# A second attention of five overlapped sequences: norm, transposes, roundings and maxima moved earlier in the slot, half of the masks on ScalarE

## The reference

```
hn = layernorm(x);  q, k, v = hn @ wq + bq, hn @ wk + bk, hn @ wv + bv      # 16 heads of 8
scores = q k^T / sqrt(8);  attn = softmax(scores);  o = attn @ v
x = x + (o @ wo + bo)
hn2 = layernorm(x);  logits = hn2 @ gate_w + gate_b;  idx = argmax(logits)
```

## Time and profile before

| | us |
|---|---|
| three runs, median (lowest to highest) | 1882.75 (1875.11 to 1886.69) |
| the profiled execution: time, span | 1882.32, 1880.5 |
| second attention, first query/key/value product to the end of its last stage | about 1226 to 1684 of the span |
| mean length of the 12 full slots (1299.6 to 1623.2) | 26.97 |

### The profile page before, as it was taken

The page is one execution under the profiler, slowest core; times in us unless marked ns, Lnnn a source line. Parts: engine busy times, 40 slices in busy tenths (PEclk is TensorE's granted clock), DMA queues, the critical chain, the costliest instruction groups (busy, mean ns, idle before and its releaser), DMA issues.

```text
span 1880.5 us, 28307 instructions
## 1 busy us (share of the span) xinstructions
PE 1255.7 (67%) x8634; PEld 880.8 (47%) x8635; DVE 1244.0 (66%) x2728; ACT 727.4 (39%) x1190; POOL 1018.8 (54%) x1176
## 2 busy tenths in 40 slices
PE   3435333478777777877787779257767776746796
PEld 1223122236666565656665558223433333325685
DVE  6788850177787878787878873167777778743322
ACT  1101001145454454454444553036565555532221
POOL 2356576456666666666666645334445444425554
PEclk7555555578888888888888887669898889878766
DMA  4010004400000000000000000210000000001110
GB/s 132 22 27 15 13 13 81 94 7 1 8 8 8 7 6 6 6 6 6 6 3 3 7 4 6 72 33 12 19 18 16 9 17 17 7 17 44 42 40 12
DMA packets 73354, 40.91 MB, mean 22 GB/s; under 512 B 23811, under 2 KB 68716, under 8 KB 73284
## 3 DMA queue, kind: packets, MB, share of 16 engines
q1 hardware_dynamic: 50530, 24.02, 4.6%
q0 software_dynamic: 20384, 11.67, 3.1%
q10 hardware_dynamic: 2370, 4.35, 0.8%
HBM read 31.11 MB, written 23.87 MB: 29 GB/s over the span
## 4 chain that ended last, share of the span: by engine, by line
PE 33%; DVE 29%; issue 13%; POOL 13%; ACT 7%; DMA 2%; ACTq 1%; POOLq 1%; SPq 0%; DVEq 0%; another core or an unknown queue 0%
PE psum L1138 9%; PE psum L1189 5%; POOL xe_dram L570 4%; DVE terms L1766 4%; DVE o L1606 4%; PE psum L1246 3%; POOL o_inv L618 3%; DVE q_highT L1792 2%; PE psum L1166 2%; POOL got L768 2%; POOL out L777 2%; PE psum L1304 1%; DVE rden L1458 1%; PE psum L1269 1%; DVE silu_g L1700 1%
## 5 line engine op out<-in xcount | busy, mean ns | idle before, releaser
L1138 PE MATMUL psum<-v,attn 128*128 128x64 f32 x2048 | 287.8, 300 | 25.6 <-ACT aggr L870 17.1
L1138 PEld LDWEIGHTS psum<-v,attn 128*128 128x128 f32 x2048 | 271.9, 213 | 61.1 <-issue 44.2
L1766 DVE TENSOR_REDUCE terms<-psum 128x4 bf16<-128x1024 f32 x128 | 156.9, 1226 | 45.5 <-PE psum L1269 43.7
L641 POOL DMA_INDIRECT yg<-ye_dram,routel x128 | 140.1, 1095 | 60.0 <-issue 36.2
L945 ACT ACTIVATE prob<-psum 128x512 f32<-128x512 f32 x256 | 139.5, 602 | 49.7 <-PE psum L1233 45.5
L570 POOL DMA_INDIRECT xe_dram<-rows_out,route x128 | 131.8, 1030 | 39.6 <-issue 39.0
L855 ACT ACTIVATE attn<-psum 128x1024 f32<-128x1024 f32 x128 | 129.9, 1015 | 10.1 <-PE psum L1121 8.9
L1147 PE MATMUL psum<-ident,o 128*128 128x128 f32 x256 | 48.7, 353 | 117.9 <-DVE silu_g L1700 91.0
L618 POOL TENSOR_TENSOR o_inv<-o_max,minus_half 128x16 f32<-128x16 f32 x32 | 107.6, 3364 | 2.7
L658 POOL TENSOR_TENSOR v<-v,inv 128x2048 f32<-128x2048 f32 x16 | 70.7, 4418 | 59.8 <-DVE inv L1586 59.8
L1147 PEld LDWEIGHTS psum<-ident,o 128*128 128x128 f32 x256 | 39.1, 183 | 131.5 <-DVE o L1606 66.5
(11 more groups left out here) (300 smaller groups left out, 3106.5 us busy)
## 6 DMA issues: line engine op xcount, KB each, us to landing
x4n_dram<-x4n SPq DMA_DIRECT2D x16, 256.0 KB, 4.5
w<-in_w POOLq DMA_DIRECT2D x48, 64.0 KB, 2.3
x_in<-in_x SPq DMA_DIRECT2D x8, 256.0 KB, 2.9
xe_dram<-zero_rows SPq DMA_DIRECT2D x8, 256.0 KB, 3.2
x_dram<-x1s SPq DMA_DIRECT2D x8, 256.0 KB, 2.4
xe_dram<-rows_out,route POOLq DMA_INDIRECT x128, 2.1
xe<-xe_dram SPq DMA_DIRECT2D x16, 128.0 KB, 2.4
ye_dram<-ye SPq DMA_DIRECT2D x16, 128.0 KB, 2.2
```

The lines of the kernel that those rows point to most:

```text
L641: pool.indirect_dma_start(yg[fetch.p][:, j, k, :], None, ye_dram, bass.IndirectOffsetOnAxis(ap=where[:, j, K0 + k:K0 + k + 1], axis=0), bo ...
L1138: mm = pe.matmul(psum[:, 4 + j, (head % HALF) * DV:(head % HALF + 1) * DV], attn[g % RING][:, h, c * SEQ + j * P:c * SEQ + (j + 1) * P], v ...
L1766: dve.tensor_reduce(dst[:, :, 2 * m2:2 * m2 + 2], psum[:, 4:6, :].rearrange("q p (b k) -> q p b k", b=2), AX, ALU.max, negate=True).then_i ...
```

## The change

Per slot: the layer norm of the fetched sequence is taken at g 2 and 4 (DVE) in place of 5 and 7, and its transposes and `h4T` at g 5 in place of 7, now in `ring[0]`. On POOL the powers for that norm stand ahead of `end` and `tail`. The query/key/value product stands ahead of the slot's first scores, and so also ahead of `values4(tail, 3)`. DVE adds query and key for both halves first and v after them, and `qkv_out` is now signalled by the v additions. The roundings on ACT stand one g earlier, the transposes of the high parts at g 1, and on DVE the choice of the expert stands in g 1 ahead of the rest, the high copy and the masks. Four of the eight masks are made by ACT at g 2. The maxima run from g 2 on: r = 0, 1, 2, 4, 5, 7 at g 2 to 7, and 3 and 6 as second ones at g 4 and 6. The diff, cut to its core:

```diff
@@ POOL half: the block "if fetch" (inverse_deviation("var4") to x3n_made) moves from behind "if tail" to ahead of "if end"
@@ ACT half
-                    if front and g == 1:
+                    if front and g == 0:
                         act.wait_ge(s["qkv_out"], 2 * front.n)
                         act.activation(high4[:], qk4[:], ACT.Copy).then_inc(s["high4_made"], 1)
-                    if front and g == 2:
+                    if front and g == 1:
                         wait(act, s["q4_ps"], 2 * (front.n - 1))
                         act.wait_ge(s["rest4_made"], front.n)
                         act.activation(flat[:, :, MID, :], qk_flat, ACT.Copy).then_inc(s["mid4_made"], 1)
+                    if front and g == 2:
+                        act.wait_ge(s["high_out"], front.n)
+                        for m in range(HALF // 2, HALF):
+                            act.activation(q_highT[:, m, :], highT[:, 0, :], ACT.Copy, scale=head_mask[:, m:m + 1]).then_inc(s["masked_act"], 1)
+                    if fetch and g == 5:
+                        act.wait_ge(s["x4T_ps"], fetch.n)
+                        act.activation(h4T[:], ring[0][:, 0:SEQ], ACT.Identity, bias=norms[:, 1:2], scale=norms[:, 0:1]).then_inc(s["h4T_made"], 1)
-                    if fetch and g == 7:
-                        act.wait_ge(s["x4T_ps"], fetch.n)
-                        act.activation(h4T[:], ring[1][:, 0:SEQ], ...)
@@ PE half
+                    if front and g == 0:
+                        for j in range(2):
+                            b = fill4(1 - j, [(s["qkv_out"], 2 * (front.n - 1) + j + 1)], [(s["h4T_made"], front.n)] if j == 0 else [])
+                            pe.matmul(b[:, 0:3 * D], h4T[:, j * P:(j + 1) * P], w_qkv[:], start=True, stop=True).then_inc(s["qkv_ps"], 1)
                     if att:
                         scores4(att, g)
                     if tail and g == 0:
                         values4(tail, 3)
-                    if front and g == 0:
-                        ...
-                    if front and g == 2:
+                    if front and g == 1:
                         b16 = fill4(0, [(s["high_out"], front.n)], [(s["high4_made"], front.n)]).bitcast(BF16)
-                    if front and g in (3, 4, 5, 6, 7):
-                        maxima(front, (0, 1, 3, 4, 6)[g - 3])
+                    if front and g > 1:
+                        maxima(front, (0, 1, 2, 4, 5, 7)[g - 2])
+                    if fetch and g == 5:
+                        b = fill4(0, [(s["h4T_made"], fetch.n)], [(s["xn4_made"], fetch.n)])
+                        ...
-                    if fetch and g == 7:
-                        b = fill4(1, [], [(s["xn4_made"], fetch.n)])
-                        ...
-                    if front and g in (4, 6, 7):
-                        maxima(front, {4: 2, 6: 5, 7: 7}[g])
+                    if front and g in (4, 6):
+                        maxima(front, {4: 3, 6: 6}[g])
@@ DVE half
                     if front and g == 0:
-                        wait(dve, s["pv_made"], HEADS * (front.n - 2))
                         wait(dve, s["terms4_made"], 6 * (front.n - 1))
                         for j in range(2):
                             dve.wait_ge(s["qkv_ps"], 2 * (front.n - 1) + j + 1)
+                            chain.step(dve.tensor_tensor(qk4[:, :, j, :], ...))
+                        wait(dve, s["pv_made"], HEADS * (front.n - 2))
+                        for j in range(2):
+                            dve.tensor_tensor(v4[front.p][:, j, :, 0:DH], ...).then_inc(s["qkv_out"], 1)
-                    if end and g == 2:
+                    if end and g == 1:
                         for j in range(2):
                             n = chain.step(dve.max(top_b[:, j, :], logit[:, j, :]))
                         ...
+                    if front and g == 1:
+                        (rest4, highT)
+                        for m in range(HALF // 2):
+                            dve.tensor_scalar(q_highT[:, m, :], highT[:, 0, :], head_mask[:, m:m + 1], None, ALU.mult).then_inc(s["masked"], 1)
+                    if fetch and g == 2:
+                        moments(x3l[fetch.p], stats4, meanvar4, "var4")
+                    if front and g > 1:
+                        take_maxima(front, (0, 1, 2, 4, 5, 7)[g - 2])
+                    if front and g == 4:
+                        take_maxima(front, 3)
+                    if fetch and g == 4:
+                        normed(xn4, x3l[fetch.p], meanvar4, rstd4, "xn4_made")
                     if front and g == 6:
-                        take_maxima(front, 5)
+                        take_maxima(front, 6)
```

More of the change, by code:

```diff
@@ L1300, in half @@
                         values4(tail, 3)
-                    if front and g == 0:
-                        for j in range(2):
-                            b = fill4(1 - j, [(s["qkv_out"], 2 * (front.n - 1) + j + 1)], [(s["h4T_made"], front.n)] if j == 0 else [])
-                            pe.matmul(b[:, 0:3 * D], h4T[:, j * P:(j + 1) * P], w_qkv[:], start=True, stop=True).then_inc(s["qkv_ps"], 1)
                     if att and g == 1:
@@ L1783, in half @@
                         dve.sem_inc(s["logit1_out"], 1)
-                    if front and g == 1:
-                        dve.wait_ge(s["high4_made"], front.n)
-                        dve.tensor_tensor(qk4[:], qk4[:], high4[:], ALU.subtract).then_inc(s["rest4_made"], 1)
-                    if front and g == 2:
-                        dve.wait_ge(s["high_ps"], front.n)
-                        dve.tensor_copy(highT[:].rearrange("q w t -> q (w t)"), ring[0].bitcast(BF16)[:, 0:2 * SEQ]).then_inc(s["high_out"], 1)
-                        dve.wait_ge(s["high_out"], front.n)
-                        for m in range(HALF):
-                            dve.tensor_scalar(q_highT[:, m, :], highT[:, 0, :], head_mask[:, m:m + 1], None, ALU.mult).then_inc(s["masked"], 1)
-                    if tail and g == 2:
-                        divide_by_sums(tail, 1, 1)
-                    if end and g == 2:
+                    if end and g == 1:
                         for j in range(2):
@@ L1808, in half @@
                         dve.tensor_tensor(prior_b[:, 2, :], prior_b[:, 1, :], onehot_b[:, 1, :], ALU.add).then_inc(s["prior1_made"], 1)
-                    if front and g in (3, 4, 5, 6):
-                        take_maxima(front, (0, 1, 3, 4)[g - 3])
+                    if front and g == 1:
+                        dve.wait_ge(s["high4_made"], front.n)
+                        dve.tensor_tensor(qk4[:], qk4[:], high4[:], ALU.subtract).then_inc(s["rest4_made"], 1)
+                        dve.wait_ge(s["high_ps"], front.n)
+                        dve.tensor_copy(highT[:].rearrange("q w t -> q (w t)"), ring[0].bitcast(BF16)[:, 0:2 * SEQ]).then_inc(s["high_out"], 1)
+                        dve.wait_ge(s["high_out"], front.n)
+                        for m in range(HALF // 2):
+                            dve.tensor_scalar(q_highT[:, m, :], highT[:, 0, :], head_mask[:, m:m + 1], None, ALU.mult).then_inc(s["masked"], 1)
+                    if tail and g == 2:
+                        divide_by_sums(tail, 1, 1)
+                    if fetch and g == 2:
+                        wait(dve, s["x3n_made"], fetch.n - 1)
+                        dve.wait_ge(s["x3l_landed"][fetch.p], 16 * fetch.k)
+                        moments(x3l[fetch.p], stats4, meanvar4, "var4")
[3 more added lines that the diff above has]
+                        take_maxima(front, 3)
                     if end and g == 3:
@@ L1827, in half @@
                         moments(x4[tail.p], stats5, meanvar5, "var5")
-                    if front and g == 4:
-                        take_maxima(front, 2)
-                    if fetch and g == 5:
-                        wait(dve, s["x3n_made"], fetch.n - 1)
-                        dve.wait_ge(s["x3l_landed"][fetch.p], 16 * fetch.k)
-                        moments(x3l[fetch.p], stats4, meanvar4, "var4")
+                    if fetch and g == 4:
+                        dve.wait_ge(s["var4"], fetch.n)
+                        dve.wait_ge(s["rstd4"], fetch.n)
+                        wait(dve, s["x4T_ps"], fetch.n - 1)
+                        normed(xn4, x3l[fetch.p], meanvar4, rstd4, "xn4_made")
                     if tail and g == 6:
@@ L1841, in half @@
                     if front and g == 6:
-                        take_maxima(front, 5)
-                    if fetch and g == 7:
-                        dve.wait_ge(s["var4"], fetch.n)
-                        dve.wait_ge(s["rstd4"], fetch.n)
-                        wait(dve, s["x4T_ps"], fetch.n - 1)
-                        normed(xn4, x3l[fetch.p], meanvar4, rstd4, "xn4_made")
-                    if front and g == 7:
                         take_maxima(front, 6)
-                        take_maxima(front, 7)
                 if fetch or front or tail or end:
```

52 lines of the change are left out of this document (25 added, 27 removed).

## The result

The changed kernel took 1913.65 us (median of 4 runs, 1907.96 to 1917.46), the kernel before beside it 1883.11: a ratio of 1.0166, 95% interval 1.0124 to 1.0207. The forecast was 1893 with a range up to 1908, so the loss is three times the one that was forecast. The profiled execution took 1917.46, with a span of 1915.8.

A forecast was written before the change was run, and what follows sets the result against it. No engine is full, so an order of pieces bounds the slot: 27.5 against 26.63, 0.9 per slot, 10.8 for 12, on the profiled 1882.32 gives 1893.1, forecast 1893. Range 1879 to 1908, leaving out 2 in 10.

The forecast's parts named there:

- Start-up: PE and DVE from product to reduction 0: logits at 4.4, masks at 7.4, reduction 0 at 9.8, 0.6 later.
- the early start of the maxima: Maxima from g 2 on: no gain in time, reduction 0 at 9.8 though PE has its matmuls ready at g 2.
- Masks: Four masks on ACT: 0.5 each, 2.0 in all, ending at about 11, covered because reduction 4 wants them past 16.
- The order: Moved pieces over one slot: next product at 26.0 with the second half's values and key terms at full clock.
- One sum: Second half on PE: reduction 3's end at 16.7, then maximum 0.3, values 1.87, key terms 1.03, given as 20.1.
- The sum: Full slot: 26.0 to 28.2, taken as 27.5 against 26.63; 0.9 per slot, 10.8 for 12.
- a sign of being wrong: Listed signs against the forecast: reduction 0 before 9, a slot under 26.5, or a clock under 0.8.
- The clock rival: PE, high transposes to maximum 1: clock falls by 0.05, 1.0 more per slot, 12 in all, 1905; chance 22%.
- The rule on gaps: PE's clock: the skill's rule that a PE with gaps falls to the half clock, cited for the clock rival.
- The faster rival: Work leaving DVE shortens the slot by what left, 1.2 x 16 = 19, to 1863; chance 7%.

The follow-up runs named there:

- with repeats: Changed kernel with PE repeating the same scores, 4 times in all at g 2, 5 at g 3, 3 at g 7: 1866.18 us, ratio 0.9932.
- the changed kernel with repeats at g 7 alone: Changed kernel with PE repeating the same scores only at g 7, 3 times in all: 1894.20 us, ratio 1.0060.
- the best version: Kernel before with four of eight masks on ACT and scores repeated, 4 times in all at g 2, 3 at g 3, 4 at g 5 and g 7: 1857.57 us.
- the repeats at g 2 and 3: Changed kernel with PE repeating the same scores 4 times in all at g 2, 5 at g 3, none at g 7: 1876.74 us, ratio 0.9981.
- the kernel before at 26.09 a slot with the clock at 0.99: Kernel before with scores repeated, 4 times in all at g 2, 6 at g 3, 4 at g 5, 4 at g 7: 1870.42 us, ratio 0.9961.
- three extra rounds a slot: Changed kernel with the same scores run 2 times in all at g 2, 3 at g 3, none at g 7: 1907.92 us, ratio 1.0151.

## Why the prediction was wrong

- **Start-up: right in the slot read.** All marks up to reduction 1 came within 0.5. That the early start of the maxima is no early start held. On average reduction 0 is at 10.44 for the forecast's 9.8, since the clock reached into the next slot.
- **Masks: right.** Each took 0.50 (median), the four 1.70 together for 2.0, and nobody waited for them. The estimate from the Trainium skill (ScalarE: Activation LUTs, What ACT_TABLE_LOAD costs), 0.49, agrees with that.
- **The order: right in size.** Worked out at the full clock, the slot was to be 26.0; with repeats it was 25.80. At a mean clock near that of the kernel before, the changed kernel with repeats at g 7 alone has 27.92 against 26.97 there, 0.95 for the forecast's 0.9. That these two agree is in part luck, as the slow stretch lies elsewhere in the slot. At 0.99 the whole change comes to -0.15; without the masks' 0.72 (below 26.09 in the best version) the rest of it would cost about 0.6. One sum was 0.2 too long (16.7, 0.3, 1.87 and 1.03 give 19.9, not 20.1), which changes nothing here.
- **The sum: this step failed.** "The slower stretch lies in most slots where it lies in this one, so 27.3, and in one slot of five a second one", with a clock of 0.82 to 0.9. It kept the slow stretch of before in its place and put a second one into one slot of five. The runs show another: in the slot read the stretch goes from 7 to 17 after the product, where it went from 11 to 18, and lies over values, output projection and first key terms (reduction 2 at 15.37 for 13.7), a second one came in at the end of every slot, and the clock is 0.77, under the 0.8 that the prediction itself names as a sign of being wrong. The premise was read from one slot. In the kernel before the 12 slots have clocks from 0.76 to 0.94 and lengths from 25.62 to 28.89; only three stand at the 0.87 of the slot that was read. `pvT` started at 23.4, was over at 24.0 for 23.1, and the next product came at 29.9 for 27.3.
- **The clock rival: right in mechanism and place, too small.** It named the stretch from the high transposes to maximum 1 (at 11.2, forecast 11.3), and priced a fall of 0.05 at 1.0. The fall was 0.10. With 0.2 per hundredth the rival's own rule gives 2.0 for that and with the 0.9 of the order 2.9, where 2.61 was measured. That this comes near is in part luck: the price came from two slots, and from 0.99 down it is 0.17 in the changed order (3.64 for 0.22) and 0.07 in that of before (0.88 for 0.12). The chance of 22% on it was too low: the change took work from PE (1.09 of 2.20 busy, where it was 2.15) next to a place where the earlier trace rows already showed it half idle ahead of a fall of the clock. That row was read as one stretch to be kept, and not as a sign of what a longer wait would do.
- **The rule on gaps.** The Trainium skill (TensorE: Matmul & The Clock Gate, HAM oscillation) has a matmul loop that waits for DMA in every round, and each time PE falls back to the half clock. The trace agrees in the fall, twice in a slot, 1.00 to 0.50 at 1460 and again at 1476; but here VectorE and ScalarE make PE wait, and the longest single wait of the slot ahead of the fall at 1460 is 0.99.
- **The faster rival: not as told, yet not empty.** Work that left DVE did shorten the slot where nothing else was changed (0.58 a slot, 1865.31), in a kernel with DVE busy 76%. The Trainium skill (Perfetto Trace Analysis, Optimizing Scalar/DVE Operations) asks for a saturated DVE; here it was enough that the masks stood on the way to the first reduction.

Open: what share of the second slow stretch follows from the first, since the repeats at g 2 and 3 took it out of some slots and not of others; what holds the kernel before at 26.09 a slot with the clock at 0.99, where five of its slots are 25.6 and two over 27; and what the moves that no run tried alone are worth (the fetched norm, the roundings, the order of the additions, the powers on POOL).

## What to carry to other kernels

When a change lengthens a wait of PE, ask first for the granted clock of the stretch behind it, in the trace of before: where it already falls after such a wait, reckon the whole ladder behind at the lower level and put the greater chance on it. An order can be free at one clock and cost 1 us of 27 at another, and more where it brings the clock down, so compare two orders at the same clock before blaming either. Where a wait can't be shortened, repeating matmuls in it is a cheap trial; try more rather than fewer, as half of the dose could not be told from none here.

## What was not expected of the hardware

- Useless work made the kernel faster: 36 more matmuls a slot (2739 for 2305 records in 12 slots) took 3.6 us off each, 0.77 to 0.99 in clock.
- The answer is not proportional: three extra rounds a slot gave 1907.92, seven gave 1876.74, none 1913.65.
- The low clock outlasts the wait: PE was full from 1464 to 1470 with the clock at 0.50.
